# Product operands by DMA through a DRAM scratch, in seven tiles of shifted fields, instead of splits, transposes and copies on the engines

## The chip, the cores and the metric

The kernel runs on one core of one Trainium2 chip. Its time is the device time in microseconds (us) from launch to end. The engines are TensorE (PE, with its weight loads PEld), VectorE (DVE), ScalarE (ACT), GpSimd (POOL) and SyncE (SP), and 16 DMA engines move data between DRAM and SBUF. Each engine runs its own list of instructions in order and waits on semaphores.

## What is computed

512 samples, each with 39 ids. An id picks a row of 16 numbers from its field's table. Then comes a compressed interaction network with two layers of 128 outputs, summed over the 16 dimensions, and a small tower of three dense layers.

```python
e = jnp.stack([tbl_0[ids[:, 0]], ..., tbl_38[ids[:, 38]]], axis=1)      # (512, 39, 16)
x0 = xk = e
for W in (W0, W1):                                    # (39*39, 128), (39*128, 128)
    Wr = W.reshape(39, Hk, 128)
    xk = jnp.einsum('bid,bjd,ijh->bhd', x0, xk, Wr)
    outs.append(xk)
z = jnp.sum(jnp.concatenate(outs, axis=1), axis=-1)
h = jnp.concatenate([z, dense_ctx], axis=1)
h = jnp.maximum(h @ W_top1 + b_top1, 0.0)
h = jnp.maximum(h @ W_top2 + b_top2, 0.0)
y = h @ W_top3
```

In the first layer both factors are `e`, so the 39 x 39 products of fields are symmetric: 780 different pairs, with the two weights of a pair added.

## The kernel before

The samples go through in 16 blocks of 32. A block has 32 x 16 = 512 columns (sample and dimension), which is one PSUM bank. Four blocks make a group of 128 samples, for which the second layer (`layer2`, 39 matmuls, L658) and the tower run once.

**Gathers.** POOL issues 10 indirect DMAs per block (L335), each of 128 rows of 64 bytes: partition `32 f + b` gets field `10 f + q` of sample `b`. They go to one of three buffers `gathered`; the eleventh and later ones of a buffer wait until DVE has read it, and from block 2 on some also wait for products of two blocks back.

**Operands.** DVE splits the gathered block into three bf16 parts (L377, L380, L383, L386) and transposes it by 32 x 32 squares (L395) into `turned`, with the parts of a field on partitions. PE multiplies `turned` by 0/1 matrices `sel_sb` (L609): one matmul gives the first factors of all tiles (`first`, stored by ACT at L476), six give the second factors of the six tiles of 128 pairs. These copies land in three PSUM banks.

**Products.** DVE multiplies `first` by a copy (L407). ACT rounds the product to fp32r (`prod_hi`, L485), DVE takes the rest (`prod_lo`, L415), and PE adds three matmuls per tile into `sums` (L623 to L625). Squares that find no room in the six tiles go an own way (L493, L495, L421, L629).

**Second layer.** The block's sum `x1` is stored, transposed by PE (L637) and split (L509, L446). PE also makes `columns`, the fields with sample and dimension on partitions (L591), which ACT and DVE store as high and low part (L466, L429). SP spreads these by 8 DMAs per block to the diagonal blocks of `diag` (L314), runs of 160 bytes each, and PE multiplies by it (`dot`, four times three matmuls, L647 to L649); ACT stores the `dots` (L519).

**Order.** PE, ACT and DVE follow lists that `orders()` makes from tables: each item has a step number, seven steps to a block, and the list is sorted by it. SP first issues all loads of tables and weights and then serves only `diag`. POOL runs in its own order.

Of the kernel before, what the change touches and what calls it, by code (L numbers as in the profile page):

```python
# [7 lines left out]
ALU = mybir.AluOpType  # L8
# [7 lines left out]
P = 128  # L16
# [12 lines left out]
TILES = 6  # L29
LEFT = FIELDS * (FIELDS + 1) // 2 - TILES * P  # L30
QUAD = 32
H1, H2 = 512, 256


def first_of_pair():

    return [p % FIELDS for p in range(P)]


def pair_tiles():  # L40

    first = first_of_pair()
    room = {i: TILES * first.count(i) for i in range(FIELDS)}
    partners = {i: [i] if i >= LEFT else [] for i in range(FIELDS)}
    need = {i: room[i] - len(partners[i]) for i in range(FIELDS)}
    open_fields = list(range(FIELDS))
    while open_fields:
        open_fields.sort(key=lambda i: (need[i], i))  # L50
        v = open_fields.pop(0)
        wins = need[v]
        for n, w in enumerate(open_fields):
            if n < wins:
                partners[v].append(w)
            else:
                partners[w].append(v)
                need[w] -= 1
        assert 0 <= wins <= len(open_fields)
    assert all(len(partners[i]) == room[i] for i in range(FIELDS))  # L60
    tiles = []
    for _ in range(TILES):
        tiles.append([partners[i].pop() for i in first])
    return tiles


def part_row(field, part):

    return QUAD * (field // QUARTER) + part * QUARTER + field % QUARTER


def selections():


    sel = np.zeros((P, TILES + 1, P), np.float32)
    back = np.zeros((P, WIDE), np.float32)
    tiles = [first_of_pair(), *pair_tiles()]
    for n, fields in enumerate(tiles):
        for p, i in enumerate(fields):
            for part in range(3):  # L80
                sel[part_row(i, part), n, p] = 1
    for i in range(FIELDS):
        for part in range(3):
            back[part_row(i, part), i] = 1
    return sel, back


def pair_rows():


    first, none = first_of_pair(), FIELDS * FIELDS
    ij = np.full((TILES + 1, P), none)
    ji = np.full((TILES + 1, P), none)
    for t, second in enumerate(pair_tiles()):
        for p, (i, j) in enumerate(zip(first, second)):
            ij[t, p] = i * FIELDS + j
            if i != j:
                ji[t, p] = j * FIELDS + i


    for n in range(3):
        for i in range(LEFT):
            ij[TILES, FIELDS * n + i] = i * FIELDS + i
    return ij, ji
# [8 lines left out]
STEPS = TILES + 1  # L113
TENSOR = dict(first=-3.51, second=(-3.43, -3.32, -3.09, -2.19, -1.71, -0.56),
              tile=(-0.0, 1.0, 2.0, 3.0, 4.0, 6.0), sum_squares=5.68, columns=-0.86, x1=8.68,
              dot=(10.74, 10.9, 11.77, 12.05))
SCALAR = dict(first=-2.73, high=(-1.73, -1.71, -0.8, -0.66, 4.2, 4.84), squares=2.8, sums=6.9, columns=0.41,
              x1=10.57, dot=(12.12, 12.27, 13.05, 13.06))
VECTOR = dict(product=(-4.16, -4.1, -3.16, -1.71, -1.14, -0.22), low=(-2.36, -1.86, -1.18, -0.66, 2.03, 3.28),
              squares=2.5, split=(-6.51, -6.31, -5.53, -5.32, -5.15), columns=0.72, x1=8.88)  # L120
# [3 lines left out]
GROUP_TENSOR = (dict(layer2=6.22, rate=2.58, tower=(23.18, 26.7, 31.41)),  # L124
                dict(layer2=6.11, rate=2.84, tower=(24.45, 27.61, 30.02)),
                dict(layer2=6.49, rate=2.72, tower=(22.71, 30.79, 31.9)))
# [26 lines left out]
def build(nc, table, ids, w0_ij, w0_ji, w1, sel, back, ident, dense, wt1, bt1, wt2, bt2, wt3, out):  # L153
    ctx = ExitStack()
    with ctx:
# [10 lines left out]
        NPROD, NPART, NGATHER, NTURN = 5, 7, 3, 3  # L166
# [5 lines left out]
        rest = sb("rest", [P, QUARTER, DIM])  # L172
        parts = sb("parts", [P, 2, DIM // 2, QUAD, 2], BF16)
        turned = sb("turned", [P, NTURN, COLS], BF16)

        sel_f = sb("sel_f", [P, TILES + 1, P])
        sel_sb = sb("sel_sb", [P, TILES + 1, P], BF16)
        back_f = sb("back_f", [P, WIDE])
        back_sb = sb("back_sb", [P, WIDE], BF16)
        ident_f = sb("ident_f", [P, P])  # L180

        w0a = sb("w0a", [P, TILES + 1, P])
        w0b = sb("w0b", [P, TILES + 1, P])
        w0_hi = sb("w0_hi", [P, TILES + 1, P], F32R)
        w0_lo = sb("w0_lo", [P, TILES, P], F32R)

        first = sb("first", [P, 2, COLS])
        prod = sb("prod", [P, NPROD, COLS])
        prod_hi = sb("prod_hi", [P, NPART, COLS], F32R)
        prod_lo = sb("prod_lo", [P, NPART, COLS], F32R)  # L190
        square = sb("square", [P, 2, COLS])
        square_parts = sb("square_parts", [P, 2, COLS], F32R)
# [573 lines left out]
```

## Time and profile before

| | us |
|---|---|
| median of three runs (254.36 to 256.9) | 256.04 |
| the profiled execution, launch to end | 252.63 |
| its span, first to last instruction | 250.8 |
| DVE busy | 181.3 |
| ACT busy | 149.3 |
| PE busy | 203.8 |
| POOL busy | 155.8 |
| bytes moved by DMA | 9.40 MB |

A busy share is an average over the whole span. Matmuls overlap, so their busy time isn't their number times their mean. The granted TensorE clock had a mean of 0.98 of full speed.

### The profile page before, as it was taken

The page shows a single profiled execution, that of the slowest core. Times are in us where ns is not written, and L with a number is a line of the kernel's source. Part 1 is how long each engine was busy: PE and PEld are TensorE (multiplying, and loading weights), DVE is VectorE, ACT ScalarE, POOL GpSimd, SP SyncE. Part 2 cuts the span into 40 slices and gives each one's busy share as a digit, 9 for nine tenths or more (in the row PEclk, how much of TensorE's full clock was granted, in tenths as well). Part 3 has the DMA queues.
Part 4 walks back from the last instruction along what each step waited for, and adds up shares of the span by engine and source line. Part 5 has one row for each costly group of instructions (what it writes and reads, how often), then busy time and mean ns, then how long its engine had stood idle before and what let it go on. Part 6 is the DMA issues. An engine that isn't in the chain of part 4 may idle for free.

```text
span 250.8 us, 3931 instructions
## 1 busy us (share of the span) xinstructions
PE 203.8 (81%) x1198; PEld 161.4 (64%) x1212; DVE 181.3 (72%) x335; ACT 149.3 (60%) x284; POOL 155.8 (62%) x165
## 2 busy tenths in 40 slices
PE   0074965786669798999898979999989699998896
PEld 0041423655447586888685868887758588887795
DVE  1463997969697979797989788979888797951000
ACT  2022645676648685678487747595968385966102
POOL 4877777777777777777777777777777870000000
PEclk9999999799958999999999999999999999999999
DMA  6993021202021212121212121212121110010000
GB/s 173 310 287 84 6 29 11 33 8 33 9 29 10 32 11 28 13 28 13 28 14 28 15 23 16 27 14 25 16 25 16 23 19 14 13 28 4 0 3 0
DMA packets 27495, 9.40 MB, mean 37 GB/s; under 512 B 22497, under 2 KB 25569, under 8 KB 27474
## 3 DMA queue, kind: packets, MB, share of 16 engines
q1 hardware_dynamic: 22354, 7.86, 14.2%
q0 software_dynamic: 5120, 1.29, 6.9%
q8 instruction: 10, 0.16, 0.3%
q14 instruction: 11, 0.09, 0.1%
HBM read 6.50 MB, written 0.00 MB: 26 GB/s over the span
## 4 chain that ended last, share of the span: by engine, by line
POOL 50%; PE 19%; issue 18%; DMA 6%; DVE 5%; ACT 1%; POOLq 0%; DVEq 0%
POOL gathered L335 50%; DMA gathered<-table,rows 5%; PE tower L658 4%; PE copies L609 2%; PE ring L647 1%; PE ring L649 1%; PE ring L648 1%; DVE turned L395 1%; DVE prod L407 1%; PE sums L623 1%; PE sums L625 1%; PE sums L624 1%; DMA ids_sb<-ids 1%; PE tower L674 1%; DVE parts L386 1%
## 5 line engine op out<-in xcount | busy, mean ns | idle before, releaser
L335 POOL DMA_INDIRECT gathered<-table,rows x160 | 155.5, 972 | 50.9 <-issue 46.9
L415 DVE TENSOR_TENSOR prod_lo<-prod,prod_hi 128x512 fp32r<-128x512 f32 x96 | 65.4, 695 | 1.8 <-ACT prod_hi L485 1.8
L407 DVE TENSOR_TENSOR prod<-first,copies 128x512 f32<-128x512 f32 x96 | 63.9, 681 | 2.1 <-ACT first L476 1.3
L485 ACT CAST prod_hi<-prod 128x512 fp32r<-128x512 f32 x96 | 58.4, 625 | 9.4 <-DVE prod L407 9.2
L609 PE MATMUL copies<-turned,sel_sb 128*128 128x512 bf16 x98 | 36.5, 411 | 24.0 <-DVE turned L395 23.2
L658 PE MATMUL tower<-dots,w_sb 128*128 128x128 f32 x312 | 47.9, 276 | 3.2 <-DVE turned L395 2.8
L658 PEld LDWEIGHTS tower<-dots,w_sb 128*128 128x128 f32 x312 | 45.7, 191 | 5.0 <-issue 1.1
L623 PE MATMUL sums<-prod_hi,w_hi 128*128 128x512 f32 x96 | 46.7, 487 | 0.3 <-DVE prod_lo L415 0.2
L519 ACT COPY dots<-ring 128x320 f32<-128x320 f32 x64 | 43.5, 748 | 5.8 <-PE ring L649 4.8
L625 PE MATMUL sums<-prod_hi,w_lo 128*128 128x512 f32 x96 | 38.6, 402 | 0.0
L624 PE MATMUL sums<-prod_lo,w_hi 128*128 128x512 f32 x96 | 38.4, 400 | 0.0
L476 ACT COPY first<-copies 128x512 f32<-128x512 f32 x16 | 9.4, 586 | 43.9 <-remote 28.4
L609 PEld LDWEIGHTS copies<-turned,sel_sb 128*128 128x128 bf16 x112 | 10.1, 100 | 39.3 <-DVE turned L395 29.3
L647 PE MATMUL ring<-diag,turned_hi 128*128 128x320 f32 x64 | 25.9, 405 | 0.4 <-ACT dots L519 0.4
L377 DVE CAST parts<-gathered 128x160 bf16<-128x160 f32 x16 | 4.3, 268 | 27.6 <-DMA gathered<-table,rows 27.6
L625 PEld LDWEIGHTS sums<-prod_hi,w_lo 128*128 128x128 f32 x96 | 18.5, 192 | 4.3
L623 PEld LDWEIGHTS sums<-prod_hi,w_hi 128*128 128x128 f32 x96 | 18.9, 197 | 3.3 <-DVE prod_lo L415 1.1
L648 PE MATMUL ring<-diag,turned_hi 128*128 128x320 f32 x64 | 20.6, 322 | 0.0
L649 PE MATMUL ring<-diag,turned_lo 128*128 128x320 f32 x64 | 20.6, 321 | 0.0
L624 PEld LDWEIGHTS sums<-prod_lo,w_hi 128*128 128x128 f32 x96 | 18.7, 195 | 1.8
L647 PEld LDWEIGHTS ring<-diag,turned_hi 128*128 128x128 f32 x64 | 12.9, 202 | 4.6 <-issue 1.8
L446 DVE TENSOR_TENSOR turned_lo<-ring,turned_hi 128x512 fp32r<-128x512 f32 x16 | 10.8, 674 | 5.6 <-ACT turned_hi L509 5.6
(85 smaller groups left out, 226.8 us busy)
## 6 DMA issues: line engine op xcount, KB each, us to landing
gathered<-table,rows POOLq DMA_INDIRECT x160, 2.4
diag<-columns SPq DMA_DIRECT2D x128, 20.0 KB
wt_sb<-wt SPq DMA_DIRECT2D x2, 512.0 KB, 6.4
sel_f<-sel SPq DMA_DIRECT2D x1, 448.0 KB, 3.3
w0a<-w_ij SPq DMA_DIRECT2D x1, 448.0 KB, 4.6
w0b<-w_ji SPq DMA_DIRECT2D x1, 448.0 KB, 5.5
ids_sb<-ids SPq DMA_DIRECT2D x1, 85.0 KB, 1.9
ident_f<-ident SPq DMA_DIRECT2D x1, 64.0 KB, 3.5
```

Source lines behind the costliest of these rows:

```text
L335: pool.indirect_dma_start(gathered[0:n, k % NGATHER, q, :], None, table, bass.IndirectOffsetOnAxis(ap=rows[0:n, k, q:q + 1], axis=0)).then ...
L407: nc.vector.tensor_tensor(prod[:, m % NPROD, :], first[:, k % 2, :], copies[n % 3][:], ALU.mult)\
L415: nc.vector.tensor_tensor(prod_lo[:, m % NPART, :], prod[:, m % NPROD, :], prod_hi[:, m % NPART, :], ALU.subtract).then_inc(lo_ready, 1)
L485: nc.scalar.copy(prod_hi[:, m % NPART, :], prod[:, m % NPROD, :]).then_inc(hi_ready, 1)
L519: nc.scalar.copy(dots[:, g % 2, :, at:at + SUB].rearrange("p i b -> p b i"), ring[n % 2][:, 0:SUB * WIDE].rearrange("p (b i) -> p b i", i= ...
L609: pe.matmul(copies[n % 3][:], sel_sb[:, e, :], turned[:, k % NTURN, :], start=True, stop=True).then_inc(copied, 1)
L623: pe.matmul(to, w0_hi[:, t, :], hi, start=(t == 0), stop=False)
L624: pe.matmul(to, w0_hi[:, t, :], lo, start=False, stop=False)
L625: pe.matmul(to, w0_lo[:, t, :], hi, start=False, stop=(t == TILES - 1)).then_inc(tile_used, 1)
L647: pe.matmul(to, hi, diag[:, k % 2, s, 0, :], start=True, stop=False)
L648: pe.matmul(to, hi, diag[:, k % 2, s, 1, :], start=False, stop=False)
L658: mm = pe.matmul(tower[:, 0:GROUP], w1_sb[:, i, :], dots[:, g % 2, i, :], start=(i == 0), stop=(i == FIELDS - 1))
```

## The change

The operands of the products no longer come through DVE, PE and PSUM. When a block's ten gathers have landed, SP writes `gathered` to a scratch `fields` in DRAM, in which a row is a field with its 512 columns (2 KB), in runs of 64 bytes: `turn_fields`, two DMAs, the second repeating 20 fields at the end of the first 40. Then `load_pairs` reads it back in eight DMAs of 117 rows of 2 KB (239.6 KB each): `first`, fields 0 to 38 three times over, and for each of seven tiles `second`, three runs of 39 fields, each shifted by one against the last. A pair is field `i` with field `i + shift`, modulo 40; tile `t` holds shifts `3 t` to `3 t + 2`. Squares are shift 0, so the separate squares go.

Tiles are 117 pairs high and seven in number, where they were 128 and six. DVE multiplies two SBUF tensors. `columns` is a transpose of `first` on PE. The PSUM banks of the copies are given to `ring` (four where there were two). `diag` is laid out so that a placing DMA has 16 runs of 1,280 bytes. Gathers have four buffers and wait only for the scratch write of four blocks back; every one has 128 rows. The load of the second layer's weights (2.5 MB) and of two tower weights (0.5 MB each) is moved behind the pair loads of blocks 0 to 2. The tables of the orders are new.

```diff
+TILES = 7
+RUN = 3
+PAIRS = RUN * FIELDS
+WRAP = FIELDS + 1
+SCRATCH = 60
...
+STEPS = TILES
+TENSOR = dict(columns=-0.5, tile=(2.3, 3.3, 4.3, 5.3, 6.3, 7.3, 8.3), x1=9.7, dot=(11.6, 11.8, 12.1, 12.6))
...
+        fields = nc.dram_tensor("fields", (BLOCKS, SCRATCH, COLS), F32, kind="Internal").ap()
...
+            def turn_fields(k):
+                slot, row = k % NGATHER, k * SCRATCH * COLS
+                sp.wait_ge(block_in[slot], 16 * QUARTER * (k // NGATHER + 1))
+                to = [[DIM, P], [4 * COLS, QUARTER], [1, DIM]]
+                again = [[DIM, P], [4 * COLS, QUARTER // 2], [1, DIM]]
+                sp.dma_start(bass.AP(fields.tensor, row, to), gathered[:, slot, :, :]).then_inc(fields_in[k % 2], 16)
+                sp.dma_start(bass.AP(fields.tensor, row + WRAP * COLS, again), gathered[:, slot, 0:QUARTER // 2, :])\
+                    .then_inc(fields_in[k % 2], 16)
+
+            def load_pairs(k):
+                at, row = k % 2, k * SCRATCH * COLS
+                sp.wait_ge(fields_in[at], 32 * (k // 2 + 1))
+                if k >= 2:
+
+                    sp.wait_ge(prod_ready, TILES * (k - 1))
+                    sp.wait_ge(ring_full, ring_no["columns", k - 2] + 1)
+                sp.dma_start(first[:, at, :],
+                             bass.AP(fields.tensor, row, [[0, RUN], [COLS, FIELDS], [1, COLS]])).then_inc(first_in[at], 16)
+                for t in range(TILES):
+                    sp.dma_start(second[:, at, t, :],
+                                 bass.AP(fields.tensor, row + RUN * t * COLS, [[COLS, RUN], [COLS, FIELDS], [1, COLS]]))\
+                        .then_inc(second_in[t][at], 16)
...
+            for k in range(BLOCKS):
+                turn_fields(k)
+                if k:
+                    place_columns(k - 1)
+                load_pairs(k)
+                load_weights(k)
+            place_columns(BLOCKS - 1)
...
             for k in range(BLOCKS):
                 if k >= NGATHER:
 
-                    pool.wait_ge(parts_ready, k - NGATHER + 1)
+                    pool.wait_ge(fields_in[k % 2], 32 * ((k - NGATHER) // 2 + 1))
...
             def product(k, t):
                 m = TILES * k + t
-                n = copy_no["second", k, t]
-                dve.wait_ge(first_ready, k + 1)
-                dve.wait_ge(copied, n + 1)
+                if t == 0:
+                    dve.wait_ge(first_in[k % 2], 16 * (k // 2 + 1))
+                dve.wait_ge(second_in[t][k % 2], 16 * (k // 2 + 1))
                 if m >= NPROD:
 
                     dve.wait_ge(lo_ready, m - NPROD + 1)
-                nc.vector.tensor_tensor(prod[:, m % NPROD, :], first[:, k % 2, :], copies[n % 3][:], ALU.mult)\
+                nc.vector.tensor_tensor(prod[:, m % NPROD, :], first[:, k % 2, :], second[:, k % 2, t, :], ALU.mult)\
                     .then_inc(prod_ready, 1)
```

SP's queue in the kernel before ends with these rows: the last loads of the start, then 128 placing DMAs and the output.

```order
L301 DMA wt_sb<-wt 128x4x256
L302 DMA wt_sb<-wt 128x2
L303 DMA bt_sb<-bt 128x4
L304 DMA bt_sb<-bt 128x2
L305 DMA w_sb<-w 128x39x128
L314 DMA diag<-columns 16x8x40 x128
L319 DMA out<-y 1x512
```

In the changed kernel the same queue, in the middle of the program, reads so for two blocks; the words in brackets are what the instruction waits for.

```order
L247 DMA fields<-gathered 128x10x16 [waits block_in1]
L248 DMA fields<-gathered 128x5x16
L286 DMA diag<-columns 16x320 [waits ring_full,ring_low]
L286 DMA diag<-columns 16x320 x7
L258 DMA first<-fields 117x1x512 [waits ring_full,prod_ready,fields_in1]
L261 DMA second<-fields 117x1x512 x7
L247 DMA fields<-gathered 128x10x16 [waits block_in2]
L248 DMA fields<-gathered 128x5x16
L286 DMA diag<-columns 16x320 [waits ring_full,ring_low]
```

The queue that held 8 DMAs per block now holds 18, and the scratch writes of a block stand behind the pair loads of the block before it and ahead of its own.

On DVE, between two blocks of the kernel before, stand the five instructions that make the operands, and what is left of the last block's products.

```order
L407 TENSOR_TENSOR prod<-first,copies 128x512
L377 CAST parts<-gathered 128x8x20
L380 TENSOR_TENSOR rest<-gathered,parts 128x8x10x2
L429 TENSOR_TENSOR columns<-ring,columns 128x4x39
L383 CAST parts<-rest 128x8x20
L386 TENSOR_TENSOR parts<-rest,parts 128x8x20
L395 STREAM_TRANSPOSE turned<-parts 128x8x32
L446 TENSOR_TENSOR turned_lo<-ring,turned_hi 128x512
```

In the changed kernel DVE goes straight from one block's products to the next's; `columns` comes behind the first product of the new block.

```order
L340 TENSOR_TENSOR prod<-first,second 117x512
L348 TENSOR_TENSOR prod_lo<-prod,prod_hi 117x512
L357 TENSOR_TENSOR columns<-ring,columns 128x4x39
L340 TENSOR_TENSOR prod<-first,second 117x512
L348 TENSOR_TENSOR prod_lo<-prod,prod_hi 117x512
```

The splits and the transpose are gone, and the first thing a block asks of DVE is a product, whose two operands come by DMA.

## Rows read from the trace of the kernel before

**Rows 1.** The page's head and its first part, engines busy.

```profile
span 250.8 us, 3931 instructions
PE 203.8 (81%) x1198; PEld 161.4 (64%) x1212; DVE 181.3 (72%) x335; ACT 149.3 (60%) x284; POOL 155.8 (62%) x165
```

**Rows 2.** The page's chain that ended last, by engine.

```profile
POOL 50%; PE 19%; issue 18%; DMA 6%; DVE 5%; ACT 1%; POOLq 0%; DVEq 0%
```

**Rows 3.** Timeline (start, duration), POOL: first, tenth and last gather.

```profile
3.31 1.10 POOL L335 DMA_INDIRECT gathered<-table,rows  x1 [2.44 <-DVE rows L343]
...
15.37 0.92 POOL L335 DMA_INDIRECT gathered<-table,rows  x1 [0.30 <-issue]
...
206.31 0.92 POOL L335 DMA_INDIRECT gathered<-table,rows  x1 [0.30 <-issue]
```

**Rows 4.** Costliest groups: count | busy us, mean ns | idle before, releaser.

```profile
L335 POOL DMA_INDIRECT gathered<-table,rows x160 | 155.5, 972 | 50.9 <-issue 46.9
L415 DVE TENSOR_TENSOR prod_lo<-prod,prod_hi 128x512 fp32r<-128x512 f32 x96 | 65.4, 695 | 1.8 <-ACT prod_hi L485 1.8
L407 DVE TENSOR_TENSOR prod<-first,copies 128x512 f32<-128x512 f32 x96 | 63.9, 681 | 2.1 <-ACT first L476 1.3
L485 ACT CAST prod_hi<-prod 128x512 fp32r<-128x512 f32 x96 | 58.4, 625 | 9.4 <-DVE prod L407 9.2
L609 PE MATMUL copies<-turned,sel_sb 128*128 128x512 bf16 x98 | 36.5, 411 | 24.0 <-DVE turned L395 23.2
L624 PE MATMUL sums<-prod_lo,w_hi 128*128 128x512 f32 x96 | 38.4, 400 | 0.0
```

**Rows 5.** Timeline, all engines, last block and end.

```profile
208.62 0.24 DVE L377 CAST parts<-gathered 128x160 bf16<-128x160 f32 x1 [2.23 <-DMA gathered<-table,rows]
...
226.46 0.58 ACT L501 COPY x<-sums 128x512 f32<-128x512 f32 x1 [0.17 <-PE sums L625]
...
231.65 1.26 ACT L519 COPY dots<-ring 128x320 f32<-128x320 f32 x2 [0.30 <-PE ring L649]
...
249.27 0.31 SPq L319 DMA_DIRECT2D out<-y  x1
```

**Rows 6.** The page's DMA queues: packets, MB, share of 16 engines over the span.

```profile
q1 hardware_dynamic: 22354, 7.86, 14.2%
q0 software_dynamic: 5120, 1.29, 6.9%
```

**Rows 7.** The page's DMA issues: count, KB each, median us to landing.

```profile
gathered<-table,rows POOLq DMA_INDIRECT x160, 2.4
diag<-columns SPq DMA_DIRECT2D x128, 20.0 KB
ids_sb<-ids SPq DMA_DIRECT2D x1, 85.0 KB, 1.9
```

**Rows 8.** DMA view, 0 to 20 us: rate in 40 slices, mean rate, queue 1.

```profile
GB/s 0 0 0 72 181 172 308 355 203 176 184 308 330 312 334 296 357 398 369 351 307 297 258 259 213 251 329 310 286 270 287 292 278 280 294 262 286 271 287 283
DMA packets 4120, 5.15 MB, mean 258 GB/s; under 512 B 1375, under 2 KB 2287, under 8 KB 4120
q1 hardware_dynamic: 3833, 5.08, 90.2%
```

**Rows 9.** DMA view, 60 to 73 us, queue 1 (placing DMAs only).

```profile
q1 hardware_dynamic: 1127, 0.16, 7.9%
```

**Rows 10.** DMA view, 249 to 250.8 us: the output's single row of 2 KB.

```profile
DMA packets 2, 0.00 MB, mean 1 GB/s; under 512 B 1, under 2 KB 1, under 8 KB 2
```

**Rows 11.** Timeline, SP: eight placing DMAs issued.

```profile
32.09 5.23 SPq L314 DMA_DIRECT2D diag<-columns  x8
```

**Rows 12.** Windows: busy us (count) by engine, PEclk, DMA share, GB/s.

```profile
41.00:44.00 3.00, 0.99 (x5) 0.47 (x3) 1.15 (x5) 1.27 (x3) 2.39 (x3) 1.00 0.11 7
44.00:50.00 6.00, 4.81 (x18) 3.83 (x19) 5.87 (x11) 3.62 (x7) 4.48 (x6) 0.72 0.26 33
102.00:115.00 13.00, 12.76 (x84) 10.80 (x84) 11.14 (x22) 9.07 (x17) 9.95 (x11) 1.00 0.19 21
```

More of the change, by code:

```diff
@@ L67, in part_row @@
[L67 to L85, printed above, removed]
@@ L88, in pair_rows @@
-def pair_rows():
[L91 to L103, printed above, removed]
+    tiles = []
+    for t in range(TILES):
+        tile = []
+        for p in range(PAIRS):
+            i, shift = p % FIELDS, RUN * t + p // FIELDS
+            j = (i + shift) % WRAP
+            tile.append(None if j == FIELDS or (shift == WRAP // 2 and i >= WRAP // 2 - 1) else (i, j))
+        tiles.append(tile)
@@ new lines, in pair_tiles @@
+    pairs = [tuple(sorted(x)) for tile in tiles for x in tile if x]
+    assert len(pairs) == len(set(pairs)) == FIELDS * (FIELDS + 1) // 2
+    return tiles
+def pair_rows():
+    none = FIELDS * FIELDS
+    ij = np.full((TILES, PAIRS), none)
+    ji = np.full((TILES, PAIRS), none)
+    for t, tile in enumerate(pair_tiles()):
+        for p, pair in enumerate(tile):
+            if pair:
+                i, j = pair
+                ij[t, p] = i * FIELDS + j
+                if i != j:
+                    ji[t, p] = j * FIELDS + i
@@ L104, in pair_rows @@
     return ij, ji
 NMLP = 4
[L113 to L120, printed above, removed]
@@ L124 @@
[L124 to L126 removed]
+STEPS = TILES
+TENSOR = dict(columns=-0.5, tile=(2.3, 3.3, 4.3, 5.3, 6.3, 7.3, 8.3), x1=9.7, dot=(11.6, 11.8, 12.1, 12.6))
+SCALAR = dict(columns=-0.2, high=(0.6, 1.6, 2.6, 3.6, 4.6, 5.6, 6.6), sums=9.1, x1=10.1,
+              dot=(12.0, 12.5, 13.1, 13.5))
+VECTOR = dict(product=(0.0, 0.9, 1.9, 2.9, 3.9, 4.9, 5.9), low=(1.2, 2.2, 3.2, 4.2, 5.2, 6.2, 7.2), columns=0.3, x1=10.7)
@@ L235, in build @@
         block_in = [sem(f"block_in{i}") for i in range(NGATHER)]
+        fields_in = [sem(f"fields_in{i}") for i in range(2)]
+        first_in = [sem(f"first_in{i}") for i in range(2)]
+        second_in = [[sem(f"second_in{n}_{i}") for i in range(2)] for n in range(TILES)]
         diag_in = [sem(f"diag_in{i}") for i in range(2)]
@@ L737 @@
     for f in range(4):
-        n = min(QUARTER, FIELDS - QUARTER * f)
-        of = np.asarray(ids)[:, QUARTER * f:QUARTER * f + n]
-        indices[f, :, :BLOCKS, :n] = of.reshape(BLOCKS, BLOCK, n).transpose(1, 0, 2)
-        indices[f, :, BLOCKS, :n] = starts[QUARTER * f:QUARTER * f + n]
-    sel, back = selections()
+        for q in range(QUARTER):
+            of = min(4 * q + f, FIELDS - 1)
+            indices[f, :, :BLOCKS, q] = np.asarray(ids)[:, of].reshape(BLOCKS, BLOCK).T
+            indices[f, :, BLOCKS, q] = starts[of]
     ij, ji = pair_rows()
```

276 lines of the change are left out of this document (79 added, 197 removed).

## The prediction

> **What bounds the kernel now.** I read the page's busy times, the chain, the timeline of POOL, the groups, the timeline of the end, and then the DMA views. By the busy times no engine is full: PE 81%, DVE 72%, POOL 62% of 250.8 us [rows 1]. The chain shows who sets the pace: half of the span is POOL and another 18% is "issue" [rows 2]. A gather takes 972 ns, and before nearly each of them stand 0.3 us of issue (46.9 us in all) [rows 4]. The first starts at 3.31 us, the tenth at 15.37 us, the last of 160 at 206.31 us [rows 3]: (206.31 - 3.31) / 159 = 1.28 us each, 12.8 us per block. So all before 208.6 us is the gathers' time and all else lies beside it. The last block is read at 208.62 us; its last `dots` are stored at 231.65 + 1.26 = 232.9 us, and the last group's second layer and tower take the 17.9 us left [rows 5].
>
> **What the change takes away.** DVE loses four splits, a transpose and a half square, and gains a product and a remainder (681 and 695 ns [rows 4]); ACT loses `first` and two square steps and gains a rounding of 625 ns; PE loses seven copies and gains three matmuls of 400 ns [rows 4]. DVE stands at 181.3 / 16 = 11.3 us per block, PE at 12.7 and ACT at 9.3 [rows 1]; each gets lighter by 1 to 2 us, and since the gathers hold the pace at 12.8 us, I cost it at nothing. The cover is POOL; were it gone the gain would be the 2 us of PE. The gathers keep their count, price and start. Before block 4 none waits; later ones wait for a scratch write of four blocks back, which costs nothing while that chain keeps up.
>
> **What it adds.** Per block: 1,920 runs of 64 bytes to DRAM, then eight loads of 239.6 KB, 1,917 KB in all, 30.7 MB over the kernel where all DMA was 9.4 MB. Two questions decide.
>
> *How many of the 16 DMA engines carry a load.* The page counts 22,354 packets on SP's queue [rows 6]. The contiguous source runs of all its transfers add up to 20,081 (16,384 for `diag`, 1,248 for `w1`, 2,449 for the rest). The 2,273 left over are 142 x 16 + 1: one small packet per engine used for each of the 142 transfers whose outer count is 128, 32 or 16, and a single one for the output, which has one row. The output's window has indeed 2 packets, one small, one of 2 KB [rows 10]. So a transfer is dealt out by its outer count and may use one engine only. The new loads read `[[.., 3], [512, 39], [1, 512]]`: three groups of 39 rows, into 117 partitions. If equal shares are cut along the outer count of both sides, three is the most that 3 and 117 allow. No transfer of before has such a shape, so the rows leave open whether it is 3 engines or more; that all counts with 16 as a divisor gave 16 and that 1 gave 1 fits equal shares. I take three.
>
> The Trainium skill, "DMA: Bandwidth & Descriptors", section "Why a DMA increments its semaphore by 16 and not by 1", says just this: the engine count is the largest up to 16 that divides the slowest dimension that is not 1 on both sides, and its rules for kernel authors warn of a leading zero-stride broadcast of c copies, which is confined to c engines. By that rule it is three and the sum below holds; without it the spread case below would have the larger part. The packet count agrees, for 16 and 1 only.
>
> *The rate of one engine.* In the first 20 us the best half microsecond moves 398 GB/s over 16 engines, 24.9 GB/s each [rows 8]. Upper price: queue 1 moved 5.08 MB in 90.2% of 16 x 20 us, 17.6 GB/s while busy [rows 8]. That was 16 engines crowding each other; three alone are nearer to the best slice. 639 KB / 24.9 GB/s = 25.7 us per block (36.3 at 17.6).
>
> By the Trainium skill, same page, "Specifications", an engine gives about 27 GiB/s, 29 GB/s; then the loads would take 22.0 us and the sum below would be 59 us less, near 505. No row shows it; the slice decides.
>
> **The cycle.** SP's order is scratch write k, placing of k - 1, loads k [the order shown above]. Write k is issued behind the loads of k - 1 and its runs on the three engines come after them in their queues. Loads k wait for `fields_in`, so for that write. So the loads of two blocks never overlap, and a block costs in series:
> - loads 25.7 us;
> - gathers that share these engines: 6.9% of 250.8 us over 16 blocks = 1.1 us [rows 6];
> - scratch write: 120 runs per engine. Nearest row: 1,127 packets of mostly 160 bytes in 7.9% of 16 x 13 us, 14.6 ns each [rows 9]: 1.8 us. Upper: the gathers' packets, 277 us / 5,120 = 54 ns [rows 6]: 6.5 us. Those hold several rows each, so I take the lower; a write to DRAM of 64 bytes is in no row.
> - turn-around, the write's receipt and the start of the next load: one landing of 2.4 us as a gather has; `ids`, 85 KB, landed in 1.9 with 0.3 of transfer, so 1.6 at least; two full landings, 4.8, at most [rows 7].
>
> Sum 31.0 us, against 12.8 now. The eight placing DMAs (5.23 us to issue [rows 11]) fall inside the loads of the block before, since `columns` needs `first` and one product only. PE needs 12.7 us a block and, at half clock, 25: still inside. The wait on `second_in` holds DVE's later products and remainders, thus `tile_used`, ACT's roundings and PE's list; all are queued behind the loads and will wait about two thirds of the time. POOL runs four blocks ahead, then waits for the scratch write.
>
> **Sum.** First block gathered: 15.37 + 0.92 + 2.4 = 18.7 us. 16 x 31.0 = 496. The 3.6 MB of weights moved between the loads, at 258 GB/s [rows 8]: 14. Loads end at 529. Behind the last tile: product, rounding, remainder, three matmuls 3.2 us (0.68 + 0.62 + 0.70 + 1.2 [rows 4]), then from the store of `x1` to the last `dots` 232.9 - 226.5 = 6.4 [rows 5]; then 17.9. The granted clock was 1.00 at 102 to 115 us with PE busy 12.76 of 13, and 0.72 of full speed at 44 to 50 us, behind 3 us in which PE was busy 0.99 [rows 12]; that is a stretch at 1.2 GHz, 0.28 x 2 x 6 = 3.4 us of it. PE will mostly wait, so I add 4 us at the end. 529 + 3.2 + 6.4 + 17.9 + 4 = 560 us of span. The profiled execution lies 1.8 us above its span (252.63), and the median of the runs 1.3% above that: 562 to 569, so **565 us**.
>
> Its own bounds: the write at 54 ns gives + 76, the turn-around + 38 or - 13, the rate of 17.6 GB/s + 170, an overlap of write and turn-around with the loads - 67. They won't all fall together: 495 to 670.
>
> **Rivals.**
> - *Three engines (0.84)*: above.
> - *The loads are spread and hidden (0.10), the other side: not slower.* From n engines on with 1917 / (24.9 n) + 5.3 below 12.8 us, n = 11, for instance 13, which divides 117, or 16, the gathers set the pace again. Then the end decides: 208.6 + write 1.8 + 2.4 + 2.4 + loads 4.8 (398 GB/s) to 7.4 (258 GB/s) puts the last tile at 220.0 to 222.6, + 9.7 = 229.7 to 232.3 where it was 232.9. Profiled 249.4 to 252.0, median about 253: on the border of faster and same. For it: nothing in the rows has an outer count of 3. Against it: the packet count.
> - *Spread, but the round trip is longer than the gathers (0.04).* Loads 7.4, gathers 1.1, write 6.5, turn-around 2.4 = 17.4 us; 278 + 18.7 + 14 + 31.5 = 342, about 345. It needs the high price of small writes. SP's own 18 issues of 0.65 [rows 11], 11.8 us, just stay below 12.8.
> - *Anything else (0.02).*
>
> **How the numbers follow.** A measurement of this kernel tells about 1% from no change. Faster comes only from half of the spread case (0.05), same from its other half (0.05), slower from the rest (0.90). The range is that of the likeliest case, 495 to 670, which holds most of its 0.84; the others lie far below, and reaching for 0.06 more isn't worth 150 us of width.
>
> **What would show it.** Loads: time to landing of a `second` growing over the eight of a block to about 28 us; DMA share near 3/16 = 0.19 at 60 to 75 GB/s, with no more engines busy; small packets of SP's queue three per load. POOL: gathers of later blocks wait, about 31 us from block to block. DVE: most idle time before L340, released by the DMA of `second`. The scratch write's landing tells the price of its runs: near 30 us when it queues behind loads. It would be wrong if the DMA share stood above 0.4 with POOL still at 1.28 us per gather; then the engine count was the failed step. If the cycle is of the right kind but not 31 us, it is the rate or the small writes.

## The result and the profile after

| | before | after |
|---|---|---|
| median, us | 256.24 (4 runs) | 595.06 (593.85 to 596.0, 4 runs) |
| span of the profiled execution, us | 250.8 | 592.0 |
| ratio | | 2.332, interval 2.321 to 2.343 |

The changed kernel takes 2.33 times as long; 565 us were predicted, with a range of 495 to 670.

The page of the changed kernel: span, busy times, the DMA queues, the chain, the costliest groups (busy, mean ns, then the idle time before and its releaser) and the DMA issues.

```profile
span 592.0 us, 3817 instructions
PE 285.3 (48%) x1132; PEld 219.6 (37%) x1132; DVE 168.1 (28%) x267; ACT 137.9 (23%) x252; POOL 154.1 (26%) x164
q1 hardware_dynamic: 54310, 39.94, 22.1%
SPq 86%; PE 4%; DMA 4%; issue 3%; POOL 2%; ACT 1%; DVE 0%; DVEq 0%
L310 POOL DMA_INDIRECT gathered<-table,rows x160 | 153.9, 962 | 254.1 <-DMA fields<-gathered 205.7
L340 DVE TENSOR_TENSOR prod<-first,second 117x512 f32<-117x512 f32 x112 | 77.6, 693 | 380.4 <-issue 194.8
fields<-gathered SPq DMA_DIRECT2D x16, 80.0 KB, 10.1
```

Against [rows 1, 2, 4, 6]: DVE and ACT work less than before in absolute terms, as the diff says. PE is busy longer, 285.3 us against 203.8, with fewer matmuls (1,132 against 1,198): its granted clock had a mean of 0.72 here and 0.98 before. POOL's gathers cost what they did (962 ns against 972), but POOL now waits 205.7 us for scratch writes. DVE is idle for 380.4 us ahead of its products. The chain has gone from POOL 50% to SP's queue 86%. SP's queue moved 39.94 MB where it moved 7.86.

One block on SP's queue and on DVE, from the timeline (start, duration, idle before):

```profile
299.41 0.76 SPq L258 DMA_DIRECT2D first<-fields  x1
300.21 15.60 SPq L261 DMA_DIRECT2D second<-fields  x7
315.86 3.18 SPq L247 DMA_DIRECT2D fields<-gathered  x1
319.08 6.63 SPq L248 DMA_DIRECT2D fields<-gathered  x1
325.82 7.31 SPq L286 DMA_DIRECT2D diag<-columns  x8
333.24 0.76 SPq L258 DMA_DIRECT2D first<-fields  x1
...
322.54 0.69 DVE L340 TENSOR_TENSOR prod<-first,second 117x512 f32<-117x512 f32 x1 [1.33 <-DMA second<-fields]
325.75 0.69 DVE L340 TENSOR_TENSOR prod<-first,second 117x512 f32<-117x512 f32 x1 [1.92 <-DMA second<-fields]
329.09 0.69 DVE L340 TENSOR_TENSOR prod<-first,second 117x512 f32<-117x512 f32 x1 [2.04 <-DMA second<-fields]
342.63 0.69 DVE L340 TENSOR_TENSOR prod<-first,second 117x512 f32<-117x512 f32 x1 [12.24 <-issue]
```

This block lasts 333.24 - 299.41 = 33.8 us; the mean of the last twelve is 33.1. Second operands come 3.2 to 3.3 us apart, so a load of 239.6 KB takes 3.25 us and eight take 26. Then DVE waits 12.2 us for the first tile of the next block (the row names no releaser; what it waits for in the program is the DMA of `first` and of the first `second`). The rate of the DMA engines in 0.5 us slices from 320 to 340 us shows both parts:

```profile
GB/s 123 74 74 74 74 74 78 74 74 74 78 74 116 102 74 51 39 11 34 13 41 41 41 26 31 42 45 51 3 33 8 25 87 82 87 74 78 86 74 89
```

While loads run, the rate is 74 GB/s, flat; three times 24.7. From 327.5 to 336 us there are no loads, only the ends of the scratch write and the small placings. SP is the one that is late: it issues the scratch write's second DMA until 325.7, then the eight placings for 7.3 us (2.9 for the first, 0.6 for each of the others), and only then the next load, whose data move 2 to 3 us later. The second scratch DMA holds SP for 6.63 us because loads are queued ahead of it. In block 0, with idle queues, the same two DMAs were issued in 0.38 and 0.63 us:

```profile
18.38 0.38 SPq L247 DMA_DIRECT2D fields<-gathered  x1
18.80 0.63 SPq L248 DMA_DIRECT2D fields<-gathered  x1
```

### The profile page after: what moved, and what is told of

Its sections match the earlier page's. It is cut to its first block, busy times and chain, and to the rows that moved or that the text cites. A ratio compares the mean times of both kernels' runs of the same rounds, so it can differ in the third digit from the quotient of the medians.

```text
span 592.0 us, 3817 instructions
## 1 busy us (share of the span) xinstructions
PE 285.3 (48%) x1132; PEld 219.6 (37%) x1132; DVE 168.1 (28%) x267; ACT 137.9 (23%) x252; POOL 154.1 (26%) x164
## 3 DMA queue, kind: packets, MB, share of 16 engines
q1 hardware_dynamic: 54310, 39.94, 22.1%
## 4 chain that ended last, share of the span: by engine, by line
SPq 86%; PE 4%; DMA 4%; issue 3%; POOL 2%; ACT 1%; DVE 0%; DVEq 0%
SPq L261 41%; SPq L286 17%; SPq L248 14%; SPq L247 8%; DMA second<-fields 3%; SPq L258 2%; SPq L272 2%; PE tower L542 2%; POOL gathered L310 2%; SPq L267 1%; SPq L271 1%; SPq L274 1%; PE tower L560 0%; DMA fields<-gathered 0%; SPq L275 0%
## 5 line engine op out<-in xcount | busy, mean ns | idle before, releaser
L310 POOL DMA_INDIRECT gathered<-table,rows x160 | 153.9, 962 | 254.1 <-DMA fields<-gathered 205.7
L340 DVE TENSOR_TENSOR prod<-first,second 117x512 f32<-117x512 f32 x112 | 77.6, 693 | 380.4 <-issue 194.8
L403 ACT CAST prod_hi<-prod 117x512 fp32r<-117x512 f32 x112 | 69.2, 618 | 244.2 <-DVE prod L340 244.2
L512 PE MATMUL sums<-prod_hi,w_hi 117*128 117x512 f32 x112 | 73.5, 656 | 101.6 <-DVE prod_lo L348 101.4
L497 PE MATMUL ring<-ident_f,first 39*128 39x39 f32 x64 | 10.3, 309 | 187.7 <-DMA first<-fields 187.7
L512 PEld LDWEIGHTS sums<-prod_hi,w_hi 117*128 117x128 f32 x112 | 28.7, 256 | 132.9 <-DVE prod_lo L348 100.4
L348 DVE TENSOR_TENSOR prod_lo<-prod,prod_hi 117x512 fp32r<-117x512 f32 x112 | 76.7, 685 | 0.1
L513 PE MATMUL sums<-prod_lo,w_hi 117*128 117x512 f32 x112 | 59.3, 529 | 0.0
L514 PE MATMUL sums<-prod_hi,w_lo 117*128 117x512 f32 x112 | 58.8, 525 | 0.0
L514 PEld LDWEIGHTS sums<-prod_hi,w_lo 117*128 117x128 f32 x112 | 30.3, 271 | 8.4
L513 PEld LDWEIGHTS sums<-prod_lo,w_hi 117*128 117x128 f32 x112 | 30.9, 276 | 0.2
L531 PEld LDWEIGHTS ring<-diag,turned_hi 128*128 128x128 f32 x64 | 15.2, 237 | 1.8 <-issue 0.2
L532 PEld LDWEIGHTS ring<-diag,turned_hi 128*128 128x128 f32 x64 | 15.1, 236 | 1.3
## 6 DMA issues: line engine op xcount, KB each, us to landing
fields<-gathered SPq DMA_DIRECT2D x16, 80.0 KB, 10.1
```

The lines of the kernel that those rows point to most:

```text
L310: pool.indirect_dma_start(gathered[:, k % NGATHER, q, :], None, table, bass.IndirectOffsetOnAxis(ap=rows[:, k, q:q + 1], axis=0)).then_inc ...
L340: nc.vector.tensor_tensor(prod[:, m % NPROD, :], first[:, k % 2, :], second[:, k % 2, t, :], ALU.mult)\
L348: nc.vector.tensor_tensor(prod_lo[:, m % NPART, :], prod[:, m % NPROD, :], prod_hi[:, m % NPART, :], ALU.subtract).then_inc(lo_ready, 1)
L403: nc.scalar.copy(prod_hi[:, m % NPART, :], prod[:, m % NPROD, :]).then_inc(hi_ready, 1)
L512: pe.matmul(to, w0_hi[:, t, :], hi, start=(t == 0), stop=False)
L513: pe.matmul(to, w0_hi[:, t, :], lo, start=False, stop=False)
```

## The experiments

All are edits of the changed kernel. The medians of the kernel before beside them were 255.0 to 256.9 us. "Period" is the time from the issue of one block's `first` to the next block's, as the mean of the last twelve blocks of the trace; the first blocks, which also move weights, are left out of it.

| run | period, us | time, us | runs |
|---|---|---|---|
| changed kernel: 3 engines, 8 loads, 8 placings | 33.1 | 595.1 | 4 |
| 3 engines, 5 loads (3 left out) | 23.3 | 441.4 | 1 |
| 3 engines, placings late | 30.9 | 561.5 | 1 |
| 3 engines, 1 placing (7 left out) | 30.2 | 551.4 | 1 |
| 13 engines, 24 loads | 17.2 | 342.3 | 1 |
| 13 engines, 8 loads | 15.3 | 316.6 | 4 |
| same, placings late | 15.3 | 314.5 | 1 |
| same, 4 placings by ACT | 13.3 | 286.3 | 4 |
| same, 1 placing (7 left out) | 12.6 | 275.1 | 2, and an earlier one of 401.3 |
| 13 engines, 4 loads | 15.8 | 326.0 | 4 |
| same, placings late | 14.7 | 302.6 | 4 |
| 13 engines, 4 loads, scratch writes by ACT | 17.9 (trace of an execution of 345.0 us) | 340.2 | 5 |

### Is it the number of engines?

Same bytes and same number of DMAs, but the outer count of the source is 39, so that 13 equal shares are possible. The transposes that make `columns` grow with it from 39 to 117 rows:

```diff
-            i, shift = p % FIELDS, RUN * t + p // FIELDS
+            i, shift = p // RUN, RUN * t + p % RUN
...
-                             bass.AP(fields.tensor, row, [[0, RUN], [COLS, FIELDS], [1, COLS]])).then_inc(first_in[at], 16)
+                             bass.AP(fields.tensor, row, [[COLS, FIELDS], [0, RUN], [1, COLS]])).then_inc(first_in[at], 16)
...
-                                 bass.AP(fields.tensor, row + RUN * t * COLS, [[COLS, RUN], [COLS, FIELDS], [1, COLS]]))\
+                                 bass.AP(fields.tensor, row + RUN * t * COLS, [[COLS, FIELDS], [COLS, RUN], [1, COLS]]))\
...
-                    mm = pe.transpose(ring[n % NRING][:, WIDE * s:WIDE * s + FIELDS],
-                                      first[0:FIELDS, k % 2, P * s:P * s + P], ident_f[0:FIELDS, 0:FIELDS])
+                    mm = pe.transpose(ring[n % NRING][:, PAIRS * s:PAIRS * s + PAIRS],
+                                      first[:, k % 2, P * s:P * s + P], ident_f[0:PAIRS, 0:PAIRS])
```

> The pairs of a tile are laid out field by field (partition 3 i + n in place of 39 n + i), so that each load reads 39 groups of 3 rows instead of 3 groups of 39: same bytes, same number of DMAs, outer count 39 beside 117 partitions. Theory (a load runs on as many engines as equal shares of both outer counts allow, 3 before, 13 now): the eight loads take 1917 KB / (13 x 24.7 GB/s) = 6.0 us instead of 26, SP's 18 issues at 0.65 to 0.75 us take 12 to 13 us per block, the gathers are again what paces the kernel, 250 to 262 us. Rival (the bytes themselves, or rereading rows just written to DRAM, limit the rate to 74 GB/s whatever engines carry it): 595 us as before. Second rival (the round trip through DRAM is longer than the gathers even with spread loads): 17 us per block, about 345 us.

It took 316.6 us, 1.241 times the kernel before (1.229 to 1.252), and 278 us less than the changed kernel. The order of two dimensions was worth that. Its page and its DMA rate from 150 to 170 us:

```profile
span 314.2 us, 3817 instructions
q1 hardware_dynamic: 55590, 39.94, 46.3%
SPq 67%; PE 11%; issue 7%; POOL 6%; DMA 5%; ACT 2%; DVE 1%; DVEq 0%
GB/s 196 140 206 262 261 265 265 296 214 156 100 60 40 23 55 44 38 29 31 58 41 10 96 233 157 122 279 275 257 214 256 259 226 235 264 256 274 289 273 141
```

Loads run at about 260 GB/s instead of 74. The small packets say how many engines carried a load. The source runs of all of SP's transfers in the changed kernel add up to 51,163; 54,310 packets leave 3,147. The transfers with outer counts of 128 and 16 (171 of them) take 16 each, 2,736; the two of `w0`, 117 rows on both sides, 13 each; the output 1. What is left, 384, is 3 for each of the 128 loads. In this run the same sum leaves 4,427 - 2,763 = 1,664 = 13 x 128. So the engine count is shown, in both kernels, and the rate follows it. A count by size agrees: the traces hold 3,147 and 4,427 packets of 4 bytes on this queue.

But 316.6 us is neither the 250 to 262 of the theory nor the 345 of the second rival: with the loads spread, a block still takes 15.3 us. SP waits for the scratch write once in the whole run (1.8 us) and for gathers only in the first blocks, so what fills the 15.3 us is SP's own issuing, in which the first placings are held behind the loads.

The other way to 13 engines keeps the layout and cuts each load into three of 39 rows:

```diff
-                for t in range(TILES):
-                    sp.dma_start(second[:, at, t, :],
+                for t in range(TILES):
+                    for n in range(RUN):
+                        sp.dma_start(second[FIELDS * n:FIELDS * n + FIELDS, at, t, :],
+                                     bass.AP(fields.tensor, row + (RUN * t + n) * COLS, [[COLS, FIELDS], [1, COLS]]))\
```

> The changed kernel with each load of 117 rows cut into three DMAs of 39 rows, one per run, so the layout stays and the outer count is 39 on both sides. 24 loads per block, 34 DMAs of SP per block. Theory of the engine count: 13 engines, transfers 6 us per block; SP's issue of 34 x 0.65 to 0.75 us = 22 to 25 us paces it, 400 to 450 us. Rival of the bytes at 74 GB/s: 26 us of transfer in any case, 595 us or more.

342.3 us, under the expected range. An issue costs less here than I counted (eight placings in 4.95 us, three loads of `first` in 1.31), so 34 DMAs fit in 17 us. The bytes as such are not the limit, and the packets say 13 engines again: 58,918 - 51,163 - 2,763 = 4,992 = 13 x 384 loads.

### What a load costs

```diff
-                for t in range(TILES):
+                for t in range(4):
                     sp.dma_start(second[:, at, t, :],
...
-                dve.wait_ge(second_in[t][k % 2], 16 * (k // 2 + 1))
+                dve.wait_ge(second_in[t % 4][k % 2], 16 * (k // 2 + 1))
...
-                nc.vector.tensor_tensor(prod[:, m % NPROD, :], first[:, k % 2, :], second[:, k % 2, t, :], ALU.mult)\
+                nc.vector.tensor_tensor(prod[:, m % NPROD, :], first[:, k % 2, :], second[:, k % 2, t % 4, :], ALU.mult)\
```

> The changed kernel loading only four of the seven second operands per block (tiles 4 to 6 use those of tiles 0 to 2 again, wrong products, same work on the engines). Theory (three engines at 24.7 GB/s, 3.2 us per load, in series with a fixed gap): 16 x 3 x 3.2 = 156 us less, about 440 us. Rival (a fixed round trip or the engines' own work is a good part of the cycle): clearly less is saved, over 500 us.

441.4 us as expected. The span went from 592.0 to 439.5, 152.5 us for 48 loads, 3.2 us each. The loads are in series with a gap that doesn't depend on them.

### What is in the gap

```diff
-                for b in range(SUB):
+                for b in range(1):
                     sp.dma_start(diag[DIM * b:DIM * b + DIM, k % 2, b, :, :, :].bitcast(F32),
                                  columns[DIM * b:DIM * b + DIM, k % 2, :, :, :].bitcast(F32))\
-                        .then_inc(diag_in[k % 2], 16)
+                        .then_inc(diag_in[k % 2], 16 * SUB)
```

> The changed kernel with one placing DMA per block instead of eight (7 of 8 diagonal blocks are not written). Theory (SP is held by its full queue until the loads are nearly through, so the eight placings, 7.3 us of issue, stand between two blocks' loads): 7 x 0.6 = 4.2 us less per block, 16 x 4.2 = 67 us less, about 528 us. Rival, which is what the prediction said (placings hidden beside the loads, the gap is the scratch write's landing): no change, 590 to 597 us.

551.4 us: between the two. The placings stood in the gap, since 42 us of span went with them, but not all 67 came out, because the scratch write's landing then took part of their place: SP waits 26 us more for it, and 42 + 26 = 68. SP's waits in this run (total, times, longest), and those of the changed kernel below:

```profile
SPq L258 <- DMA fields<-gathered: 28.1, 16, 2.1
```

```profile
SPq L258 <- DMA fields<-gathered: 2.1, 1, 2.1
```

So each of the 16 blocks now waits about 1.8 us for the write; before, only the first did. Moving the placings without leaving anything out:

```diff
                 turn_fields(k)
-                if k:
-                    place_columns(k - 1)
                 load_pairs(k)
+                if k:
+                    place_columns(k - 1)
                 load_weights(k)
```

> The changed kernel (loads on three engines), nothing left out, with the placings of block k - 1 issued behind the loads of block k instead of ahead of them. Theory (with three engines SP has time to spare, and only what it issues between the end of one block's loads and the start of the next costs): the gap falls to the scratch write's landing, as it did with one placing, 545 to 560 us. Rival (the placings only move to stand ahead of the next scratch write and delay that): 590 us or more.

561.5 us, a span 32.3 us shorter, and just over the expected 545 to 560. The rival (590 or more) is out, but only 2.0 of the placings' 7.3 us per block are saved, since they now stand ahead of the next scratch write, and SP waits 3.9 us per block for its landing:

```profile
SPq L258 <- DMA fields<-gathered: 61.7, 16, 5.1
```

### Why a spread kernel is still slower than before

With one placing per block, twice:

> The field-by-field layout (loads on 13 engines) with one placing DMA per block instead of eight (7 of 8 diagonal blocks are not written). Theory (in the run with 13 engines SP's queue paces the block at 16.0 us: 6.7 for eight loads, 1.7 for two writes, 7 for eight placings): 16.0 - 7 x 0.65 = 11.4 us, below the gathers' 12.8, so about 250 to 262 us. Rival (the round trip through DRAM or the transfers pace it): 300 us or more.

> The kernel with loads on 13 engines and one placing per block again (7 of 8 diagonal blocks not written), because its first run took 401 us with matmuls of 680 ns instead of 400 to 450 from start to end. If that was the one execution's TensorE clock, it comes out at 250 to 290 us here; if it belongs to the kernel, at about 400 us again.

The first run took 401.3 us and says nothing about SP, as PE was slow in it from start to end; the last section has its rows. The second took 275.1 (two runs, 1.073 times the kernel before, 1.062 to 1.084), with 12.6 us per block, no more than the gathers take. That is not the gathers' pace: SP waits for gathers only twice, in the first blocks, and it waits for the write's landing in every block, as with three engines:

```profile
SPq L258 <- DMA fields<-gathered: 28.6, 16, 2.1
SPq L247 <- DMA gathered<-table,rows: 19.8, 2, 14.5
```

It missed the 250 to 262 expected of its first run mainly in its first three blocks. Their `first` is issued at 21.5, 37.4 and 58.8 us and that of the fourth at 75.5 us: 54.0 us, where three periods of 12.6 would be 37.9. The 16 us more go to the 3.6 MB of weights, which the change moved behind the pair loads of blocks 0 to 2, so into SP's series. In the kernel before, SP had issued all of them by 9.2 us, ahead of the first block. The gathers run ahead meanwhile, but SP can't make up for it at 12.6 us per block: its last `first` is issued at 227.2 us, 14 us after the last gather (211.8 + 0.9) has been issued. The other spread versions in which SP issues the writes lose 14 to 18 us in the same place. No run has the weights elsewhere, so what moving them back would save is read from the trace and not tested.

Nothing left out, with half of the placings issued by ACT:

```diff
-                for b in range(SUB):
+                for b in range(SUB // 2):
...
+                for b in range(SUB // 2, SUB):
+                    act.dma_start(diag[DIM * b:DIM * b + DIM, k % 2, b, :, :, :].bitcast(F32),
```

> The field-by-field layout with four of the eight placings issued by ACT, nothing left out. Theory of the full SP queue: SP needs 6.7 + 1.7 + 3.5 = 11.9 us per block, ACT 8.5 + 2.7 = 11.2 us, the gathers pace again, 250 to 262 us. Rival (ACT's issues hold back its roundings, or the transfers need about 14 us with their gap): 270 to 290 us. Whether it beats the kernel before is open: both end about 42 us behind the last gather.

286.3 us, 1.125 times the kernel before (1.111 to 1.138): the best version that leaves nothing out, in the rival's range (270 to 290) and not the theory's. The gathers are dearer here, 1,043 ns each against 972 before, and the last one starts at 217.9 us where it was 206.3:

```profile
L310 POOL DMA_INDIRECT gathered<-table,rows x160 | 166.9, 1043 | 51.5 <-issue 48.2
```

Placings late, with 13 engines:

> The field-by-field layout with the placings of block k - 1 issued behind the loads of block k instead of ahead of them. Same 18 issues per block. Theory of the full SP queue: 16.0 us per block stay, 310 to 320 us. Rival (what costs is that the placings stand between the scratch write and the loads, the transfers being idle meanwhile): 13 to 14 us per block, 265 to 285 us.

314.5 us, in the range of the theory of the full queue, and not apart from the 316.6 us without the move. But 30.8 us of it are SP's waits for the scratch write, 1.9 per block, where the theory had issues alone, so the number agrees better than the account. That theory counts issues, so it was tried with fewer of them. With shift `7 n + t`, a partition's seven rows are neighbours in the scratch, and three longer loads do for seven:

```diff
-            i, shift = p % FIELDS, RUN * t + p // FIELDS
+            i, shift = p // RUN, TILES * (p % RUN) + t
...
+                for t, end in ((0, 2), (2, 4), (4, 7)):
+                    sp.dma_start(second[:, at, t:end, :].rearrange("p t c -> p (t c)"),
+                                 bass.AP(fields.tensor, row + t * COLS,
+                                         [[COLS, FIELDS], [TILES * COLS, RUN], [1, (end - t) * COLS]]))\
```

> The field-by-field layout with shift 7 n + t instead of 3 t + n: a partition's seven second operands are then seven neighbouring rows of the scratch, and three loads of 4, 4 and 6 KB per partition take the place of seven of 2 KB. Same bytes, 13 engines, 4 loads per block instead of 8, nothing left out, all placings on SP. Theory (SP's issues pace the block once the loads are spread): SP needs 4 x 0.85 + 1.7 + 7 = 12 us per block, under the gathers' 12.8, and the transfers 7 us: 255 to 268 us. Rival (the transfers with the gap between two blocks pace it): no better than the run in which ACT shares the placings, 280 us or more.

326.0 us (1.266 times before, 1.253 to 1.279), with a period of 15.8: four issues less per block saved nothing, and the theory that the number of SP's issues sets the pace fell. Its SP timeline, with the first product of the block on DVE:

```profile
165.01 0.87 SPq L258 DMA_DIRECT2D first<-fields  x1
165.93 2.51 SPq L261 DMA_DIRECT2D second<-fields  x3
168.48 0.68 SPq L247 DMA_DIRECT2D fields<-gathered  x1
169.20 3.43 SPq L248 DMA_DIRECT2D fields<-gathered  x1
173.83 7.24 SPq L287 DMA_DIRECT2D diag<-columns  x8
181.17 0.87 SPq L258 DMA_DIRECT2D first<-fields  x1
...
172.28 0.69 DVE L341 TENSOR_TENSOR prod<-first,second 117x512 f32<-117x512 f32 x1 [2.17 <-DMA second<-fields]
...
SPq L287 <- DVE columns L358: 13.4, 12, 5.0
```

The loads are issued in 3.4 us, but the placings begin only at 173.8 and hold the next load back by 7.2 us. They wait for `columns`, which DVE stores behind the block's first product, and that product waits for the first `second`, which is now a load of two tiles: it comes 7.3 us after the issue of `first`, where it came after 5.0 us with eight loads. So the edit saved issues and made this wait longer at once (the last row: 13.4 us in 12 blocks). What counts is the series: load landed, product, `columns`, then all that SP issues before the next load. So I put fewer loads and late placings together:

> Four loads per block on 13 engines (shift 7 n + t) and the placings of block k - 1 issued behind the loads of block k. Nothing left out. Theory (SP's list is a chain: loads, placings and scratch write are issued one after another, and the next loads wait for the write's landing; what is issued beside running transfers costs nothing): with loads issued in 3.4 us, the 5 us of placings fall beside 8 to 9 us of transfer, and a block costs transfer 8.5 + write 1.5 + landing and start 3 = 13 us, close to the gathers' 12.8: 255 to 275 us. Rival (the placings, wherever they stand, hold back the scratch write and so the next loads, as in the run with seven loads and late placings): 15 to 16 us per block, 305 to 325 us.

302.6 us (1.186 times before, 1.177 to 1.196), period 14.7, just below the rival's 305 to 325 and far above the theory's range. Of each period about 3.7 us is now SP's wait for the scratch write, which was issued behind the placings and while the loads still moved:

```profile
SPq L258 <- DMA fields<-gathered: 58.8, 16, 5.2
```

Last, the writes were given to ACT's list, to come out of that series. ACT issues them between its roundings (step -2.2 of its table). In the same edit the placings of block `k` come right behind its loads:

```diff
-SCALAR = dict(columns=-0.2,
+SCALAR = dict(turn=-2.2, columns=-0.2,
...
             for k in range(BLOCKS):
-                turn_fields(k)
-                if k:
-                    place_columns(k - 1)
                 load_pairs(k)
                 load_weights(k)
-            place_columns(BLOCKS - 1)
+                place_columns(k)
```

> Four loads per block on 13 engines (shift 7 n + t), and the scratch writes of a block are issued by ACT, on its own queue, as soon as the gathers have landed; SP only issues loads and placings. Nothing left out. Theory (what was left in the other spread runs is the series of one queue: loads, then placings or scratch write, then the write's landing, 14 to 16 us per block): with the write out of the series a block costs the larger of 8.5 us of transfer and SP's 3.4 + 7 + 3 us of waiting for columns, so the gathers' 12.8 us pace it: 252 to 268 us. Rival (the sum of transfers on the engines, or the wait for columns, holds it at 14 us even so): 280 to 305 us.

340.2 us (1.322 times before, 1.307 to 1.338), worse than all spread versions but one. In the timeline of SP, ACT's queue and DVE:

```profile
184.69 0.37 ACTq L383 DMA_DIRECT2D fields<-gathered  x1
...
187.70 0.86 SPq L249 DMA_DIRECT2D first<-fields  x1
188.61 2.50 SPq L252 DMA_DIRECT2D second<-fields  x3
195.79 5.01 SPq L278 DMA_DIRECT2D diag<-columns  x8
...
194.24 0.69 DVE L329 TENSOR_TENSOR prod<-first,second 117x512 f32<-117x512 f32 x1 [5.84 <-DMA second<-fields]
```

ACT reaches the write of the next block only after roundings that need this block's operands. The write lands at 187.7, loads start, and the first product comes at 194.2. The round trip write, load, product, rounding, write is now closed through ACT's in-order list, and costs about 17 us here. The placings are done by 200.8 us and don't hold the next load, which waits for the write until 205.1. The place in ACT's table was mine and was not varied, so this shows a bad place and not that ACT can't do it.

## Why the prediction was right, point by point

**The bound before** was the gathers, and nothing found since speaks against that. The experiments don't test it: none of them is paced by the gathers, and the version with one placing has blocks of 11.7 to 13.6 us. The assumption that the gathers keep their price held with three engines (962 ns against 972) and not with 13 (992 to 1,043 ns).

**The taken work at nothing** was right in kind: DVE's busy time fell from 181.3 to 168.1 us and ACT's from 149.3 to 137.9, and DVE was idle for 380.4 us ahead of its products.

**Three engines** was right, and is shown by the packet count (384 = 3 x 128) and by turning two dimensions (3 to 13 engines, 595 to 317 us). The Trainium skill, "DMA: Bandwidth & Descriptors", "Why a DMA increments its semaphore by 16 and not by 1", gives the rule, the largest number up to 16 that divides both outer counts. By it the one shape has 3 engines and the other 13, and the runs agree with both. One reading of the working was off without harm: it counts `w1` as 1,248 source runs. It has 4,992 runs of 512 bytes, which travel in 1,248 packets of 2 KB. The number left over is right: the trace of the kernel before holds 2,273 packets of 4 bytes.

**The rate** of 24.9 GB/s per engine was taken from the best slice; it came out at 24.7 (74 / 3), 26.0 us for eight loads against 25.7 predicted. The prediction's other figure, 29 GB/s, was not reached.

**The gap** is where the sum was low. I had 1.1 for gathers, 1.8 for the write's runs and 2.4 of turn-around, 5.3 us; measured are 33.1 - 26.0 = 7.1. The step that failed is "the eight placing DMAs fall inside the loads of the block before". They would, if SP were free; but with loads queued, an issue takes as long as a load (3.18 us for a scratch DMA that then lands 10 us later), so SP reached the placings when the loads were nearly through. For the same reason the write landed in 10.1 us and not in the "near 30" of the signs: SP issued it when about half of the loads were already done. The gap of the changed kernel is thus filled by other things than the sum names, the placings and the start of the next load, while the write's landing hides behind the placings (SP waits for it once, 2.1 us). That 5.3 and 7.1 are close is in part luck. With the placings gone or moved the period is 30.2 or 30.9 us, and the 31.0 of the prediction was near the kernel without that mistake. 16 x 2.1 = 34 us covers the 32 us between the span of 560 and the 592.0 measured. The weights took 112.8 - 3 x 33.1 = 13.6 us over the first three blocks, where 14 were counted. The scratch write was rightly cheap: in block 0, with idle queues, the 80 KB and the 40 KB in runs of 64 bytes landed in 2.3 and 2.7 us.

```profile
fields<-gathered SPq DMA_DIRECT2D x1, 80.0 KB, 2.3
fields<-gathered SPq DMA_DIRECT2D x1, 40.0 KB, 2.7
```

**The end** was right: from the last tile's product to the end of the span 592.0 - 559.4 = 32.6 us, where 31.5 were counted. The granted clock was down, as expected of an engine that waits: a mean of 0.60 from 300 to 333 us, so mostly the 1.2 GHz level, with PE busy 15.24 of 33 us:

```profile
300.00:333.00 33.00, 15.24 (x45) 10.14 (x45) 9.89 (x16) 8.63 (x17) 8.68 (x10) 0.60 0.24 69
```

**The rivals.** The spread case was said to be hidden, near 253 us, from 11 engines on. The experiment that made it true gave 317. That rival's price was wrong by 60 us for two reasons. It was a sum of transfers and landings, and took SP's list for free. The list was priced at 18 issues of 0.65 us, 11.8 us, under the gathers' 12.8; measured it fills the 15.3 us, since a load costs 0.8 to 0.9 us to issue and the placings 5.8 to 7.2 us behind queued loads. 16 x 2.5 = 40 us of the 60. Most of the rest is the weights, which stand in the same series: the first three blocks take 17.6 us more than three periods. The other spread rival, 345 us, had the wrong cause, dear small writes: where little is queued ahead, the write lands in 2.3 to 2.8 us.

## What to carry to other kernels

Before a load is written as a view with a small outer count, turn the dimensions so that the first counts of both sides share a large divisor up to 16: the same bytes ran at 260 GB/s with 39 outside and at 74 with 3 outside. When a DMA depends on one that the same queue issued before it, add up the queue as a chain (transfer, what is issued behind it, landing, next start) and not as a share of time, and count an issue into a full queue at the length of a transfer. Loads that are moved off the start of a kernel into such a chain are paid for there in full (about 16 us for 3.6 MB here). Here work was taken from engines that were not the bottleneck and given to a queue that closes a round trip per block; no version that leaves nothing out came under 1.125 times the kernel before.

## What the hardware showed that I had not expected

An issue on SP into a queue full of loads takes as long as a load, 3.2 us on three engines; with 13 engines and four loads per block, three loads are issued in 2.5 us and only the second scratch DMA is held, 3.4 us.

Thirteen engines move 260 GB/s, 20 GB/s each, where three give 24.7 each; why, no run tells.

The same kernel (13 engines, one placing) took 401 us in one execution and 275 in two others. The group of the remainder's matmuls, and the window from 100 to 140 us (the third number from the end is the granted clock), first in the execution of 401 us, then in the other:

```profile
L513 PE MATMUL sums<-prod_lo,w_hi 117*128 117x512 f32 x112 | 76.2, 680 | 0.0
100.00:140.00 40.00, 40.00 (x128) 33.22 (x128) 19.36 (x32) 14.88 (x27) 30.85 (x31) 1.00 0.52 135
```

```profile
L513 PE MATMUL sums<-prod_lo,w_hi 117*128 117x512 f32 x112 | 47.6, 425 | 0.0
100.00:140.00 40.00, 36.27 (x230) 31.93 (x229) 31.26 (x53) 24.99 (x46) 31.03 (x30) 1.00 0.65 166
```

PE was busy for all 40 us of the first and 36.3 of the second, and both show a granted clock of 1.00. But back to back matmuls of 512 columns started mostly 0.44 us apart in the first, from its start to its end, and mostly 0.23 us apart in the second:

```profile
100.71 0.61 PE L513 MATMUL sums<-prod_lo,w_hi 117*128 117x512 f32 x1
101.15 0.61 PE L514 MATMUL sums<-prod_hi,w_lo 117*128 117x512 f32 x1
```

In the other runs 0.43 us goes with the lower of the two levels, 1.2 GHz. So the clock column says full speed and the matmuls say about half. The trace of this execution holds no record of a change of the clock at all, and the column then reads 1.00. The same holds at the start of the other runs, ahead of their first record: in the changed kernel that comes 83 us into the span, and until then its back to back matmuls of 512 columns start 0.43 us apart under a column of 1.00 (63.82 and 64.25 us, for one pair). A granted clock of 1.00 is worth checking against the distance of back to back matmuls. What kept PE low in that execution stays open.
